# Row-tiled attention scores, two PSUM banks a unit, in an attention and expert kernel

## What is computed

```python
x = x + xattn(layernorm(x), ctx, ctx)      # 16 heads of 8, causal mask, softmax
x = x + ffn(layernorm(x))                  # 8 experts, top 2 of each batch
# xattn: q = query @ Wq.T ; k = key @ Wk.T ; v = value @ Wv.T, in 16 heads of 8
#   attn = softmax(where(causal, q k^T * 8**-0.5, -1e9)) ; out = (attn @ v) @ Wo.T
# ffn: rw = softmax(mean over the 64 tokens @ Wr + br), top 2, their softmax
#   expert e: gelu(x @ W1[e] + b1[e]) @ W2[e] + b2[e] ; out = weighted sum of two
#   y = out + x ; return (y - mean) / sqrt(var + 1e-5) * gamma + beta
```

## Time and profile before

| | |
|---|---|
| median of 3 runs | 651.03 us |
| profiled execution | 649.7 us, span 648.0 |
| busy, share of the span | PE 92%, PEld 69%, DVE 86%, ACT 81%, POOL 67% |
| attention, about | 12.9 to 381 us |
| routing, about | 381 to 404 us |
| expert blocks, about | 404 to 607 us |
| PE clock granted, mean | 0.961 of full |

### The profile page before, as it was taken

The page is one execution under the profiler, slowest core; times in us unless marked ns, Lnnn a source line. Parts: engine busy times, 40 slices in busy tenths (PEclk is TensorE's granted clock), DMA queues, the critical chain, the costliest instruction groups (busy, mean ns, idle before and its releaser), DMA issues.

```text
span 648.0 us, 18845 instructions
## 1 busy us (share of the span) xinstructions
PE 593.4 (92%) x4465; PEld 450.3 (69%) x4465; DVE 558.6 (86%) x1538; ACT 525.3 (81%) x1163; POOL 435.2 (67%) x687
## 2 busy tenths in 40 slices
PE   4999999999999999999999924999999999999762
PEld 2677777777777777777777611788888878888652
DVE  3989999999999999999998955888888888898576
ACT  3788888888888888888888734988888888888595
POOL 5778988888888889888888774444444444454133
PEclk9999999999999999999999965899999999999787
DMA  3010100001010000101011002123322332322034
GB/s 99 26 34 11 34 24 13 27 24 32 8 32 24 18 23 24 32 8 32 8 47 34 3 1 65 51 61 94 93 62 61 94 95 61 91 58 64 26 114 146
DMA packets 55583, 30.02 MB, mean 46 GB/s; under 512 B 4856, under 2 KB 54528, under 8 KB 55552
## 3 DMA queue, kind: packets, MB, share of 16 engines
q1 hardware_dynamic: 55120, 29.47, 15.6%
q10 hardware_dynamic: 432, 0.20, 0.1%
HBM read 13.00 MB, written 4.19 MB: 27 GB/s over the span
## 4 chain that ended last, share of the span: by engine, by line
PE 86%; ACT 5%; DVE 3%; issue 3%; ACTq 1%; POOL 1%; DVEq 1%; DMA 0%; POOLq 0%
PE bank L347 17%; PE bank L359 8%; PE bank_pair L372 7%; PE bank L344 6%; PE bank L385 6%; PE bank L473 5%; PE bank L474 5%; PE bank L475 5%; PE bank_pair L486 5%; PE bank_pair L488 5%; PE bank_pair L487 5%; PE bank L333 3%; PE bank L325 2%; ACT squares L691 2%; PE bank L321 2%
## 5 line engine op out<-in xcount | busy, mean ns | idle before, releaser
L1072 POOL TENSOR_TENSOR probs<-probs,row_sum_recip 128x512 f32<-128x512 f32 x128 | 133.5, 1043 | 38.9 <-DVE row_sum_recip L789 34.9
L347 PE MATMUL bank<-k_by_head,q_by_row_group 128*128 128x256 f32 x512 | 132.3, 381 | 0.0
L1125 POOL CAST gathered<-z_hi_lo (+1 forms) x114 | 45.2, 432 | 114.4 <-PE bank L475 104.9
L670 ACT ACTIVATE gelu<-bank,b_expert 128x512 f32<-128x512 f32 x144 | 98.4, 690 | 26.3 <-PE bank L475 20.2
L580 ACT ACTIVATE probs<-scores_shifted 128x512 f32<-128x512 f32 x128 | 80.5, 629 | 38.7 <-DVE scores_shifted L783 37.9
L347 PEld LDWEIGHTS bank<-k_by_head,q_by_row_group 128*128 128x128 f32 x512 | 98.9, 193 | 14.2 <-issue 0.3
L773 DVE TENSOR_REDUCE row_max<-bank 128x8 f32<-128x512 f32 x128 | 87.9, 687 | 17.3 <-PE bank L347 14.3
L905 DVE SCALAR_TENSOR_TENSOR zT_then_yT<-bank_pair,slot_weight,zT_then_yT x288 | 74.7, 283 | 18.1 <-issue 17.4
L589 ACT ACTIVATE probsT<-bank 128x512 f32<-128x512 f32 x128 | 76.4, 597 | 13.9 <-PE bank L359 8.8
L776 DVE TENSOR_REDUCE row_sum<-probs 128x8 f32<-128x512 f32 x128 | 86.3, 674 | 0.4 <-ACT probs L580 0.2
L783 DVE TENSOR_TENSOR scores_shifted<-bank,row_max 128x512 f32<-128x512 f32 x128 | 86.5, 676 | 0.0
(11 more groups left out here) (166 smaller groups left out, 1221.8 us busy)
## 6 DMA issues: line engine op xcount, KB each, us to landing
gathered<-z_hi_lo SPq DMA_DIRECT2D x187, 64.0 KB, 1.8
x_res<-in_x SPq DMA_DIRECT2D x16, 256.0 KB, 2.7
ctxT_pair<-in_ctxT SPq DMA_DIRECT2D x32, 128.0 KB, 2.0
w_raw<-in_w SPq DMA_DIRECT2D x16, 256.0 KB, 3.0
out<-gelu SPq DMA_DIRECT2D x16, 256.0 KB, 2.2
gathered<-z_hi_lo ACTq DMA_DIRECT2D x3, 64.0 KB, 1.9
wq<-in_wq SPq DMA_DIRECT2D x1, 64.0 KB, 2.3
wk<-in_wk SPq DMA_DIRECT2D x1, 64.0 KB, 2.2
```

The costliest lines, as they stand in the source:

```text
L347: mm = nc.tensor.matmul(ps[:, 256 * rp:256 * rp + 256], QR[:, par, s, 2 * rp:2 * rp + 2, :].rearrange("p a k -> p (a k)"), KM[:, par, s, : ...
L670: nc.scalar.activation(G[:, c, :], bank[c][:, :], ACT.Gelu, bias=b1e).then_inc(a_g if c == 0 else a_gp, 1)
L1072: nc.gpsimd.tensor_tensor(pp, pp, RC[:, k % 2, :].unsqueeze(2).to_broadcast([128, 8, S]), ALU.mult).then_inc(g_norm, 1)
```

## The change

1. Scores: q stays as it is, QT [128, 2, 4, 64]; four products, each on 32 rows by 64 columns of the array (row group r, column half r % 2), write to half r % 2 of the partitions of bank r // 2. A unit has two banks with 256 columns each, the mask is written by two products of 256 columns, and p_s counts four a unit. The eight banks are now: two pairs for scores, one for turned probabilities, one for attend, J0, J1.
2. PE's order in a step: mask(u), turn(u-3), scores(u), attend(u-4). `turn` waits for ACT's copy of the unit just before; `attend` of an even unit for the copy of the two before.
3. V for 128 tokens at a time: two products of 128 columns; ACT places it with four copies rather than two. q needs one copy rather than four, and no zeros.
4. The shifts are made on POOL in `rstd`: negation of the mean beside the add, and a product after the power.
5. x + beta goes from attention to POOL's expert loop, one 256-column piece in each of the first 32 blocks.

```diff
@@ -127,7 +127,7 @@
...
-            QR = early("q_by_row_group", [128, 2, 4, 4, S])
+            QT = early("qT", [128, 2, 4, S])
...
@@ -141,7 +141,7 @@
...
             identb = early("ident_bf", [128, 128], BF16)
-            cmask = early("causal_mask", [128, 8, S], BF16)
+            cmask = early("causal_mask", [128, 4, S], BF16)
...
@@ -163,12 +163,14 @@
...
-        bank = [es.enter_context(nc.psum_tensor(f"bank{n}", [128, 512], F32)) for n in range(4)]
+        SP2 = [es.enter_context(nc.psum_tensor(f"scores_banks{n}", [128, 2, 512], F32)) for n in range(2)]
+        bank = [SP2[n // 2][:, n % 2, :] for n in range(4)]
...
         bank += [es.enter_context(nc.psum_tensor(f"bank{n}", [128, 512], F32)) for n in (6, 7)]
-        S_ps, T_ps, A_ps, J0, J1 = bank[0:2], bank[2:4], bank[4:6], bank[6], bank[7]
-        B2Y = A_ps[1][:, 0:128]
+        T_ps, A_ps, J0, J1 = bank[4], bank[5], bank[6], bank[7]
+        S_ps = [SP2[n][:, :, 0:256] for n in range(2)]
+        B2Y = bank[5][:, 0:128]
...
@@ -328,35 +330,38 @@
...
                 ge(pe, a_v, P)
-                for b in range(4):
-                    for j2 in range(2):
-                        mm = nc.tensor.matmul(J1[64 * j2:64 * j2 + 64, 64 * b:64 * b + 64],
-                                              CT[:, par, 64 * b:64 * b + 64], WV[:, j2, :], start=True, stop=True)
+                for t in range(2):
+                    mm = nc.tensor.matmul(J1[:, 128 * t:128 * t + 128], CT[:, par, 128 * t:128 * t + 128],
+                                          WV[:, :, :].rearrange("p j n -> p (j n)"), start=True, stop=True)
...
+            def mask(i, k):
+
+                ge(pe, v_sub, 8 * i + k - 1)
+                for rp in range(2):
+                    nc.tensor.matmul(S_ps[k % 2][:, rp, :], identb[:, :], cmask[:, :, :].rearrange("p a k -> p (a k)"),
+                                     start=True, stop=False, skip_group_check=True)
...
-                U, P, s, par, ps = 8 * i + k, 2 * i + k // 4, k % 4, k // 4 % 2, S_ps[k % 2]
+                P, s, par, ps = 2 * i + k // 4, k % 4, k // 4 % 2, S_ps[k % 2]
...
                     ge(pe, g_km, P + 1)
-                ge(pe, v_sub, U - 1)
-                nc.tensor.matmul(ps[:, :], identb[:, :], cmask[:, :, :].rearrange("p a k -> p (a k)"),
-                                 start=True, stop=False, skip_group_check=True)
-                for rp in range(2):
-                    mm = nc.tensor.matmul(ps[:, 256 * rp:256 * rp + 256],
-                                          QR[:, par, s, 2 * rp:2 * rp + 2, :].rearrange("p a k -> p (a k)"),
-                                          KM[:, par, s, :, :].rearrange("p a k -> p (a k)"),
+                for r in range(4):
+                    rows = slice(32 * r, 32 * r + 32)
+                    mm = nc.tensor.matmul(ps[64 * (r % 2):64 * (r % 2) + 64, r // 2, :], QT[rows, par, s, :],
+                                          KM[rows, par, s, :, :].rearrange("p a k -> p (a k)"),
                                           start=False, stop=True, skip_group_check=True)
-                mm.then_inc(p_s, 1)
+                    mm.then_inc(p_s, 1)
...
                 ge(pe, g_norm, U + 1)
-                ge(pe, a_pt, U - 1)
+                ge(pe, a_pt, U)
                 for b in range(4):
-                    mm = nc.tensor.transpose(T_ps[k % 2][:, 128 * b:128 * b + 128],
+                    mm = nc.tensor.transpose(T_ps[:, 128 * b:128 * b + 128],
...
@@ -366,10 +371,10 @@
...
                 if s % 2 == 0:
-                    ge(pe, a_at, T - 1)
+                    ge(pe, a_at, T)
...
                 for b in range(4):
-                    mm = nc.tensor.matmul(A_ps[k // 2 % 2][32 * b:32 * b + 32, 128 * (k % 2):128 * (k % 2) + 128],
+                    mm = nc.tensor.matmul(A_ps[32 * b:32 * b + 32, 128 * (k % 2):128 * (k % 2) + 128],
...
@@ -402,9 +407,11 @@
...
                     if not static or U < NB:
-                        scores(i, u)
+                        mask(i, u)
...
                         turn(i, u - 3)
+                    if not static or U < NB:
+                        scores(i, u)
...
@@ -525,10 +532,12 @@
...
                 for j2 in range(2):
-                    rows = slice(64 * j2, 64 * j2 + 64)
-                    ins = nc.scalar.activation(VM[rows, par, :, :, j2, :].rearrange("p b g d -> p (b g) d"),
-                                               J1[rows, 0:256].rearrange("p (n d) -> p n d", d=HD), ACT.Copy)
-                    ins.then_inc(a_vh if j2 == 0 else a_v, 1)
+                    for odd in range(2):
+                        ins = nc.scalar.activation(
+                            VM[64 * j2:64 * j2 + 64, par, :, :, j2, :].rearrange("p (t o) g d -> p o t g d", o=2)[:, odd],
+                            J1[64 * odd:64 * odd + 64, 0:256].rearrange("p (t j g d) -> p j t g d", t=2, j=2, d=HD)[:, j2],
+                            ACT.Copy)
+                        ins.then_inc(a_v if j2 + odd == 2 else a_vh, 1)
...
@@ -539,15 +548,13 @@
...
                 act.wait_ge(p_q, P + 1)
-                ge(act, p_s, 4 * P - 4)
-                for r in range(4):
-                    rows = slice(32 * r, 32 * r + 32)
-                    nc.scalar.activation(QR[rows, par, :, r, :], J0[rows, 0:256].rearrange("p (b q) -> p b q", q=S),
-                                         ACT.Copy).then_inc(a_q if r == 3 else a_qp, 1)
+                ge(act, p_s, 16 * P - 16)
+                nc.scalar.activation(QT[:, par, :, :].rearrange("p b q -> p (b q)"), J0[:, 0:256],
+                                     ACT.Copy).then_inc(a_q, 1)
...
-                act.wait_ge(v_sh1, P + 1)
+                act.wait_ge(g_sh1, P + 1)
...
@@ -719,17 +726,6 @@
...
-
-            def shift1(P):
-                dve.wait_ge(g_rs1, P + 1)
-                nc.vector.scalar_tensor_tensor(SH1[:, :], MV1[:, :, 0], -1.0, RS1[:, :],
-                                               ALU.mult, ALU.mult).then_inc(v_sh1, 1)
-
-            def shift2(P, h):
-
-                dve.wait_ge(g_rs2, P + 1)
-                nc.vector.scalar_tensor_tensor(SH2[:, :], MV2[:, 2 * h:2 * h + 2, 0], -1.0, RS2[:, :],
-                                               ALU.mult, ALU.mult).then_inc(v_sh2, 1)
...
@@ -768,9 +764,10 @@
...
                     if now:
-                        ps = S_ps[u % 2][:, :].rearrange("p (n k) -> p n k", k=S)
-                        dve.wait_ge(p_s, U + 1)
-                        nc.vector.reduce_max(MX[:, u % 2, :], ps, AX.X).then_inc(v_max, 1)
+                        ps = S_ps[u % 2].rearrange("p r (n k) -> p r n k", k=S)
+                        mx = MX[:, u % 2, :].rearrange("p (r n) -> p r n", r=2)
+                        dve.wait_ge(p_s, 4 * U + 4)
+                        nc.vector.reduce_max(mx, ps, AX.X).then_inc(v_max, 1)
...
@@ -792,19 +789,14 @@
...
                         stats1(P + 2)
-                    if s == 2 and (not static or P + 2 < NP):
-                        shift1(P + 2)
...
                         zsum(P - 3)
-                    if s == 3 and (not static or 0 <= P - 2 < NP):
-                        shift2(P - 2, h)
...
             stats1(0)
-            nc.vector.memset(QR[:, :, :, :, :], 0.0).then_inc(v_setup, 1)
-            shift1(0)
+            dve.nop().then_inc(v_setup, 1)
...
@@ -1012,29 +1003,32 @@
...
                 for q0 in (0, 64):
-                    keep(cmask[q0:q0 + 64, :, :], ALU.is_ge, 0, [[0, 8], [-1, S]], 1, MASKED)
+                    keep(cmask[q0:q0 + 64, :, :], ALU.is_ge, 0, [[0, 4], [-1, S]], 1, MASKED)
...
-            def rstd(mv, rs, eps_sem, rs_sem, n):
-
-                nc.gpsimd.tensor_tensor(rs, mv, eps[:, 0:rs.shape[-1]], ALU.add).then_inc(eps_sem, 1)
-                pool.wait_ge(eps_sem, n)
-                nc.gpsimd.tensor_tensor(rs, rs, minus_half[:, 0:rs.shape[-1]], ALU.pow).then_inc(rs_sem, 1)
+            def rstd(P, mv, rs, sh, eps_sem, rs_sem, sh_sem):
+
+                nc.gpsimd.tensor_tensor(rs, mv[:, :, 1], eps[:, 0:2], ALU.add).then_inc(eps_sem, 1)
+                nc.gpsimd.tensor_scalar(sh, mv[:, :, 0], -1.0, None, ALU.mult).then_inc(eps_sem, 1)
+                pool.wait_ge(eps_sem, 2 * P + 2)
+                nc.gpsimd.tensor_tensor(rs, rs, minus_half[:, 0:2], ALU.pow).then_inc(rs_sem, 1)
+                pool.wait_ge(rs_sem, P + 1)
+                nc.gpsimd.tensor_tensor(sh, sh, rs, ALU.mult).then_inc(sh_sem, 1)
...
                 ge(pool, a_xn, P)
-                rstd(MV1[:, :, 1], RS1[:, :], g_eps1, g_rs1, P + 1)
+                rstd(P, MV1[:, :, :], RS1[:, :], SH1[:, :], g_eps1, g_rs1, g_sh1)
...
                 ge(pool, a_z, P)
-                rstd(MV2[:, 2 * h:2 * h + 2, 1], RS2[:, :], g_eps2, g_rs2, P + 1)
+                rstd(P, MV2[:, 2 * h:2 * h + 2, :], RS2[:, :], SH2[:, :], g_eps2, g_rs2, g_sh2)
...
                 pool.wait_ge(a_xk, P + 1)
-                ge(pool, p_s, 4 * P - 4)
+                ge(pool, p_s, 16 * P - 16)
...
```

(38 more changed lines are left out.)

5 lines of the change are left out of this document (2 added, 3 removed).

## The result

| | before | after |
|---|---|---|
| median of the runs | 651.53 us (650.01 to 652.18) | 659.00 us (657.13 to 659.91) |
| ratio to before, 95% interval | | 1.0113 [1.0089, 1.0137] |
| profiled execution | 649.7, span 648.0 | 659.9, span 658.1 |
| a pair, mean of 21 in a row between 90 and 335 us | 11.25 | 11.44 |

The change makes the kernel 1.1% slower. The forecast was 642.4 us, a gain of 1.3%, with a range of 627 to 658. The means of a pair in the experiments are taken in the same stretch, over 20 to 22 pairs.

The account below looks back on a forecast made before the run. PE's own work bound attention before; a loop through PE, DVE and POOL would after. 0.24 a pair over 30 pairs (-7.2), start -1.0, end -0.4: 649.7 to 641.1, plus 1.3 for the median: 642.4 us, range 627 to 658.

Parts of the forecast that it names:

- rival B: PE's scores: tiles sharing output columns take turns, scores 0.87 us, loop 11.9 a pair, 668 us; chance 0.12.
- The loop: Attention: a chain of steps through PE, DVE and POOL sets the pair at 11.05 us, against 11.29 before.
- Turn to turn: PE, from the turn of s = 0 to the next unit's turn: 3.04 us, mask and scores included.
- all four tiles at once: PE's scores: the four row tiles run together, eight instructions costing 2 x 0.217 = 0.43 us.
- Scores to DVE: From the start of the s = 1 scores to DVE's maximum: 0.43 + 0.165 drain + 0.05 us.
- rstd with shift: POOL, between the s = 1 product and the spread: 1.36 us, against 0.94 without the shift.
- Rival D: POOL's small operations cost their upper bound: 11.33 a pair; with slower two-bank DVE reads 11.53, 655 us; chance 0.12.
- Hand-over to PE: From the end of POOL's s = 2 product to PE's turn of s = 0: 0.08 us.
- Start: Kernel start: shift ready 0.65 us earlier, q copy shorter, V copies longer; -1.0 us, bounds 0 and -2.
- End: At the end, with the shift no longer held on DVE: -0.4 us.
- Expert blocks: Expert stage: x + beta on POOL is covered by its idle time before the gather, costing zero.
- Rival C: PE's scores overlap only partly, with switches at full drain: 11.34 a pair, 649.6 to 651 us, no change; chance 0.10.

Follow-up runs that it names:

- e9: Kernel after, with POOL's rstd1 (with its shift) moved from step s = 1 to s = 0: 633.97 us, ratio 0.9726.
- e3: Kernel after, with x + beta back in attention, in POOL's step s = 0: 657.39 us, ratio 1.0105.
- e8: Kernel after, with one count a unit on the last scores product instead of four: 655.01 us, ratio 1.0067.
- e1: Kernel after, with scores put ahead of turn again in PE's order: 637.78 us, ratio 0.9799.
- e5: Kernel before, with only PE's order changed to mask, turn, scores, attend: 656.96 us, ratio 1.0093.
- e6: Kernel before, with PE's order mask, turn, scores, attend and the shifts on POOL: 669.71 us, ratio 1.0290.
- e12: Kernel before, with only x + beta moved from attention to POOL's expert loop: 651.46 us, ratio 1.0002.

## Why the prediction was wrong

**What held.** PE bound before, in attention. The new order makes the loop the bound; its path, its waits and the fact that x + beta lies outside are as predicted, and e9, e3, e8 and e1 show it: taking 1.41 us out of the loop gave 0.87 a pair and 25 us, until POOL's own work came up, and 0.7 more beside it cost nothing. Row tiles do run four at a time. Instructions of L353 at work in the kernel after, scores of s = 1 starting at 210.91:
```profile
210.92:210.94 0.02, 0.02 (x4) 1.00 0.00 0
...
211.14:211.16 0.02, 0.02 (x4) 1.00 0.00 0
211.16:211.18 0.02, 0.02 (x5) 1.00 0.00 0
211.18:211.20 0.02, 0.02 (x8) 1.00 0.00 0
```
Four start within 0.02 us and the other four some 0.27 after them, where the 256 columns of one instruction cost 0.217. The whole step, from the first start to attend's, is 0.59 and not 0.87 or more, so rival B is out. The Trainium skill's 3.07 times for four row tiles (TensorE: Matmul & The Clock Gate, Measured speedup vs the span model) makes an estimated 0.57 of one after another's 1.74; this trace's 0.59, with the change of shape in it, is close to that.

**What failed: the term "The loop", 11.05 a pair, measured 11.41.** The margin against PE's 11.29 was 0.24, and the loop's own terms were off by 0.36, all to one side:
- Turn to turn, +0.12. Half is the scores: to attend they took 0.59 (207.81 to 208.40), priced as 0.43 + 0.10. The second round comes 0.05 late, and behind it stand 0.32, its 0.217 and 0.10 for the change of shape. So the 0.10 was right and the 0.43 was not: the term that was mis-sized is "all four tiles at once" without a gap between the rounds. The rule that the prediction named (the Trainium skill, TensorEngine Tiling (Array Packing), Key Properties: a change of tiling mode drains TensorE) would put 0.165 behind the scores where 0.10 stands; with the 0.05 between the rounds it comes to 0.16, but no run tells whether that 0.05 belongs to the change of shape. The other half is the turn behind a wait, 207.22 to 207.81 = 0.59 against 0.53; e5 and e6 missed by it too.
- Scores to DVE, +0.16: 0.66 from first start to last end where 0.43 + 0.165 was taken, 0.05 of it the late round again, and 0.15 of hand-over where 0.05 was. Half of the term is the four counts, +0.08, shown by e8. The diff showed one semaphore counting four a unit and the prediction gave it no price.
- rstd with shift, +0.05: 1.41 for 1.36. Rival D's upper bound was not needed. Hand-over to PE, +0.02, and DVE's part, +0.01.

So the loop lies above PE's old pace, not below it: +0.19 a pair in place of -0.24. Over the attention stage that is +7.5 us against -7.2, 14.7 of the 18.8 us by which the profiled execution missed the sum.

**The small terms.** Start, -1.0: measured -0.85, by luck. The first norm began at 6.96, since POOL's power took 1.58 and not 0.71:
```profile
5.07 1.58 POOL L1014 TENSOR_TENSOR ln_rstd<-ln_rstd,minus_half 128x2 f32<-128x2 f32 x1
5.09 0.91 DVE L803 MEMSET v_blocks<- 128x1024 f32 x1 [0.28 <-DVE mask_r L802]
```
DVE's memset beside it doesn't explain that, since in e8 the same two stand side by side and the power takes 0.72:
```profile
5.02 0.72 POOL L1014 TENSOR_TENSOR ln_rstd<-ln_rstd,minus_half 128x2 f32<-128x2 f32 x1
5.04 0.91 DVE L803 MEMSET v_blocks<- 128x1024 f32 x1 [0.28 <-DVE mask_r L802]
```
The cause is open. End, -0.4: measured +1.9, of which one part is PE's clock, granted 0.57 of full from 380 to 384 us, for most of it the lower of its two levels (1.2 GHz); the last four transposes took 1.12 us there and 0.66 before.
```profile
380.64 1.12 PE L364 MATMUL bank_pair<-ident,probs 128*128 128x128 f32 x4 [0.77 <-POOL probs L1065]
```
PE had stood waiting for POOL just before, the 0.77 of this row. It waited before the change too, 0.69 ahead of its last transposes at 373.42, and had the full clock from 372 to 376 us; why the clock fell earlier now was not tested, nor how the 1.9 splits. Expert blocks, 0: +2.2 in this execution, within the spread told at e12.

**The chances.** The range ended 1 us below the median. The forecast's own ends were 10.6 to 11.27 a pair. Rival C, given 0.10, came nearest in mechanism and length: rounds that come late and full drains, 11.34, to which the 0.05 of rstd adds up to 11.39, no gain. What the prediction held against it, that attend's two rounds are 0.11 apart, is a misreading: in the trace of before, the attend that starts at 200.84 has its fifth instruction only after 200.96, so the second round comes some 0.13 after the first. That much was to be had beforehand; the counts and the turn behind a wait stood in no rival. Rival D's sum was also off: 11.53 a pair gives 657 by the prediction's own terms, not 655.
